# A four-layer graph network: ranking by source and the first node stage with their work in another order

## The reference

```python
h_in = relu(layernorm(x))                      # then the layer's own products
# layer 0
h_raw = h_in @ W.T + b
h_dir = h_raw / max(norm(h_raw), 1e-12)
h     = h_dir * sigmoid(h_in @ mag_w.T + mag_b) * 1.5
scores = h[src] @ a_s + h[tgt] @ a_t           # one number an edge
ex  = exp(scores - segment_max(scores, tgt)[tgt])
agg = segment_sum(h[src] * ex / (segment_sum(ex, tgt)[tgt] + 1e-10), tgt)
h   = ball_projection(h + agg)
```

## Time and profile before

| | |
|---|---|
| median of three runs | 9786.06 us |
| profiled execution, its span | 9778.72 us, 9777.0 us |
| busy share of the span | PE 62%, DVE 58%, POOL 50%, ACT 32% |
| granted TensorE clock, mean | 0.80 of full speed |
| first node stage | about 130 to 929 us of the span |
| ranking by source | about 933 to 2129 us |

### The profile page before, as it was taken

The page is one execution under the profiler, slowest core; times in us unless marked ns, Lnnn a source line. Parts: engine busy times, 40 slices in busy tenths (PEclk is TensorE's granted clock), DMA queues, the critical chain, the costliest instruction groups (busy, mean ns, idle before and its releaser), DMA issues. The chain is left out here.

```text
span 9777.0 us, 155051 instructions
## 1 busy us (share of the span) xinstructions
PE 6076.9 (62%) x21338; PEld 3661.3 (37%) x21339; DVE 5653.9 (58%) x19482; ACT 3099.9 (32%) x10799; POOL 4876.5 (50%) x5997
## 2 busy tenths in 40 slices
PE   4666877756768887677999945444003678500277
PEld 3554233324543433455666611111002557400165
DVE  4666988873558776354445455555001458755664
ACT  2665022211554443254444400000000466411046
POOL 1333177756632212664444467775666652455252
PEclk8998577777989998799999966666556999755599
DMA  2332000004876654596666632332002797411057
GB/s 84 134 132 96 0 1 1 1 1 151 284 256 215 214 206 173 181 302 233 236 234 234 222 98 90 91 90 66 1 0 76 234 302 217 144 42 42 23 178 229
DMA packets 779248, 1347.62 MB, mean 138 GB/s; under 512 B 139839, under 2 KB 546391, under 8 KB 779156
## 3 DMA queue, kind: packets, MB, share of 16 engines
q1 hardware_dynamic: 208564, 650.10, 19.0%
q10 hardware_dynamic: 413792, 410.91, 13.2%
q0 software_dynamic: 156800, 285.65, 10.5%
HBM read 751.95 MB, written 594.32 MB: 138 GB/s over the span
## 5 line engine op out<-in xcount | busy, mean ns | idle before, releaser
L1435 PE MATMUL node_p_out<-w,node_h_t 128*128 128x512 f32 (+3 forms) x7840 | 2614.7, 466 | 379.1 <-ACT node_h_t L1463 141.9
L990 PE MATMUL merge_banks<-merge_rows,merge_mask 128*128 x6264 | 1680.7, 425 | 744.0 <-SPq L959 464.5
L1435 PEld LDWEIGHTS node_p_out<-w,node_h_t 128*128 128x128 f32 x7840 | 1357.1, 197 | 1077.7 <-issue 734.9
L990 PEld LDWEIGHTS merge_banks<-merge_rows,merge_mask 128*128 128x128 f32 x6264 | 1278.1, 211 | 1146.6 <-issue 954.0
L972 DVE TENSOR_SCALAR merge_mask<-ramp,dst_at,soft_at_step 128x128 f32<-128x128 f32 x2349 | 847.2, 366 | 1069.8 <-PE merge_banks L990 950.3
L1078 POOL DMA_INDIRECT merge_rows<-h,merge_take_i x1176 | 1125.1, 957 | 655.6 <-issue 249.4
L1022 ACT COPY merge_total<-merge_banks 128x256 f32<-128x256 f32 x1568 | 577.6, 369 | 1251.5 <-PE merge_banks L990 1135.4
L1613 PE MATMUL score_table<-score_at_high,score_at_low 128*128 128x392 f32 x784 | 565.6, 827 | 588.8 <-DVE score_at_high L1574 584.0
L1009 ACT COPY merge_banks<-merge_held 128x256 f32<-128x256 f32 x1568 | 588.1, 376 | 897.5 <-DMA merge_held<-own 643.3
L1353 POOL TENSOR_TENSOR node_inv_std<-node_var,node_minus_half 128x4 f32<-128x4 f32 x392 | 437.0, 1115 | 751.0 <-DVE node_var L1311 750.0
L1463 ACT ACTIVATE node_h_t<-node_p_turn 128x256 f32<-128x256 f32 x1568 | 594.7, 385 | 349.6 <-PE node_p_turn L1413 344.9
(11 more groups left out here) (409 smaller groups left out, 9678.3 us busy)
## 6 DMA issues: line engine op xcount, KB each, us to landing
h<-node_out SPq DMA_DIRECT2D x196, 512.0 KB, 5.7
merge_held<-own ACTq DMA_DIRECT2D x196, 512.0 KB, 5.8
x<-merge_total ACTq DMA_DIRECT2D x196, 512.0 KB
node_x<-x SPq DMA_DIRECT2D x196, 512.0 KB, 5.9
node_x<-in_x SPq DMA_DIRECT2D x194, 512.0 KB
h<-node_rows_h SPq DMA_DIRECT2D x98, 512.0 KB, 2.7
merge_held<-h ACTq DMA_DIRECT2D x98, 512.0 KB
mix<-merge_total ACTq DMA_DIRECT2D x98, 512.0 KB
```

Of the source, the lines that this page charges most:

```text
L990: nc.tensor.matmul(banks[:, bass.ds(nc.s_assert_within(at[2 * j + 1], 0, (BANKS - 1) * 512, skip_runtime_bounds_check_because=small), D)], ...
L1435: ins = nc.tensor.matmul(p_out[w][g % banks][:, 0:n], h_t[g][:, c * P:(c + 1) * P], matrix[:, c, :], start=c == 0, stop=c == 1)
```

## The change

Node stage, layer 0: DVE's and ACT's stages are called tile by tile (`by_tile=True`): one tile of each stage, then the next tile of each. `normalize` comes first, then `add_bias`, then `average`. `resize` follows two steps after `measure` instead of one. The pair columns are scaled by one DVE instruction a group (`pair_tile`, L1509 after) in place of four of ACT's; SP waits for it before it stores.

Ranking: `rank_sources` takes the place of `rank_phase` with `EndSums`. The 392 low one-hots are kept from the histogram. The running starts live in one PSUM bank: PE adds into it, ACT copies it out (`snap`) before each addition. Engines work on different tiles in one step: DVE high one-hot of tile t, mask of t-2, pick of t-4; PE add of t-2, transpose of t, match of t-1, rank of t-3. POOL copies its own indices, eight tiles at once, gathers, and adds the pairs itself.

```diff
+def rank_sources(nc, k, pos_out, ends, score):
+    ph = Phase(nc, "rank_src")
...
+    p_run = ph.ps("run", [P, 512])
...
+            def hot_low(t, j):
+                nc.vector.tensor_scalar(at_low[:, bass.ds(t, 1), :].rearrange("p o f -> p (o f)"), k.ramp[:, 0:P],
+                                        columns(low, t), None, ALU.is_equal).then_inc(hist_low, 1)
+            def hot_high(t, j, done):
+                nc.vector.tensor_scalar(at_high[j][:], k.ramp[:, 0:NTH], columns(high, t), None, ALU.is_equal).then_inc(done, 1)
+            def histogram(t, j):
+                hot_low(t, j)
+                after(dve, hist_mm, t - U + 1)
+                hot_high(t, j, hist_high)
...
+            def head(t, j):
+                after(dve, ranked, t - U + 1)
+                after(dve, added, t - U + 1)
+                after(dve, picked_n, t - U + 1)
+                hot_high(t, j, high_hot)
+            def before_in_tile(t, j):
+                dve.wait_ge(same, t + 1)
+                after(dve, ranked, t - FOUR + 1)
+                nc.vector.tensor_tensor(earlier[j % FOUR][:], p_same[j % 2][:, 0:P], k.before[:],
+                                        ALU.mult).then_inc(masked, 1)
+            def pick(t, j):
+                dve.wait_ge(ranked, t + 1)
+                dve.wait_ge(high_hot, t + 1)
+                after(dve, picked_n, t - 1)
+                if j == 0 and not (isinstance(t, int) and t < U):
+                    dve.wait_ge(rank_kept, t // U if isinstance(t, int) else (t >> 3))
+                nc.vector.tensor_tensor_reduce(picked[j % 2][:], at_high[j][:], p_rank[j % 2][:, 0:NTH], 1.0, 0.0,
+                                               ALU.mult, ALU.add, rank_f[:, j:j + 1]).then_inc(picked_n, 1)
+                if j == U - 1:
+                    dve.wait_ge(picked_n, t + 1)
+                    nc.vector.tensor_copy(columns(pos_out, t - U + 1, U), rank_f[:]).then_inc(rank_kept, 1)
+            walk(dve, [(0, head), (2, before_in_tile), (4, pick)])
...
+            def add(t, j):
+                pe.wait_ge(high_hot, t + 1)
+                pe.wait_ge(snapped, t + 1)
+                nc.tensor.matmul(p_run[:, 0:NTH], at_low[:, bass.ds(t, 1), :].rearrange("p o f -> p (o f)"), at_high[j][:],
+                                 start=False, stop=False, skip_group_check=True).then_inc(added, 1)
...
+            def rank(t, j):
+                pe.wait_ge(copied, t + 1)
+                pe.wait_ge(snapped, t + 1)
+                after(pe, picked_n, t - 1)
+                nc.tensor.matmul(p_rank[j % 2][:, 0:NTH], low_t[j][:], starts[j % FOUR][:], start=True, stop=False)
+                pe.wait_ge(masked, t + 1)
+                pe.wait_ge(high_hot, t + 1)
+                nc.tensor.matmul(p_rank[j % 2][:, 0:NTH], earlier[j % FOUR][:], at_high[j][:], start=False,
+                                 stop=True).then_inc(ranked, 1)
+            walk(pe, [(2, add), (0, turn), (1, match), (3, rank)])
+        @block.scalar
+        def _(act):
+            act.wait_ge(prefix, 1)
+            def snap(t, j):
+                after(act, added, t)
+                after(act, ranked, t - FOUR + 1)
+                nc.scalar.copy(starts[j % FOUR][:], p_run[:, 0:NTH]).then_inc(snapped, 1)
+            def copies(t, j):
+                act.wait_ge(turned, t + 1)
+                after(act, same, t - FOUR + 1)
+                nc.scalar.copy(low_tb[j % FOUR][:], p_turn[j % 2][:, 0:P]).then_inc(copied_b, 1)
+                after(act, ranked, t - U + 1)
+                nc.scalar.copy(low_t[j][:], p_turn[j % 2][:, 0:P]).then_inc(copied, 1)
+            walk(act, [(2, snap), (0, copies)])
...
+            def block_of(i, half, uses):
+                at = half * U
+                nc.gpsimd.tensor_copy(take_src[:, at:at + U], columns(k.src_i, i * U, U)).then_inc(indexed, 1)
+                nc.gpsimd.tensor_copy(take_dst[:, at:at + U], columns(k.dst_i, i * U, U)).then_inc(indexed, 1)
+                pool.wait_ge(indexed, 2 * (i + 1))
+                pool.sem_inc(turn_pool, 1)
+                for j in range(at, at + U):
+                    nc.gpsimd.indirect_dma_start(of_src[:, j, :], None, ends,
+                                                 bass.IndirectOffsetOnAxis(take_src[:, j:j + 1], 0)).then_inc(got[half], 16)
+                    nc.gpsimd.indirect_dma_start(of_dst[:, j, :], None, ends,
+                                                 bass.IndirectOffsetOnAxis(take_dst[:, j:j + 1], 0)).then_inc(got[half], 16)
+            def join(i, half, uses):
+                at = half * U
+                pool.wait_ge(got[half], 16 * 2 * U * uses)
+                nc.gpsimd.tensor_tensor(columns(score, i * U, U), of_src[:, at:at + U, 0], of_dst[:, at:at + U, 1],
+                                        ALU.add).then_inc(scored, 1)
+                pool.wait_ge(scored, i + 1)
+                pool.sem_inc(turn_pool, 1)
...
+        live = []
         for lag, stage in stages:
             side = (c - lag) % S
             uses = i + (c - lag - side) // S
             H = uses * S + side
             if isinstance(H, int) and not 0 <= H < groups:
                 continue
-            stage(Group(H, side, uses, groups))
+            live.append((stage, Group(H, side, uses, groups)))
+        for g in range(G if by_tile else 1):
+            for stage, q in live:
+                stage(q, g) if by_tile else stage(q)
...
+                    sp.sem_inc(turn_sp, 1)
+                    sp.wait_ge(paired, q.H + 1)
...
+            def normalize_tile(q, g):
+                if g == 0:
+                    dve.wait_ge(std_made, q.H + 1)
+                    if not q.new:
+                        dve.wait_ge(turned, G * q.last)
+                ins = nc.vector.tensor_scalar(xn[q.h][:, g, :], x[q.h][:, g, :], moments[q.h][:, g, 0:1],
+                                              inv_std[q.h][:, g:g + 1], ALU.subtract, ALU.mult)
+                if g == G - 1:
+                    ins.then_inc(normed, 1)
+            def bias_tile(q, g):
+                if g == 0 and not q.new:
+                    dve.wait_ge(out_made, q.last)
+                    dve.wait_ge(paired, q.last)
+                dve.wait_ge(product, G * q.H + g + 1)
+                nc.vector.tensor_tensor(out[q.h][:, 0, g, :], p_out[0][g][:, 0:n_out], k.bias0[:], ALU.add).then_inc(raw_made, 1)
+            def pair_tile(q, g):
+                if g < G - 1:
+                    return
+                dve.wait_ge(scale_made, q.H + 1)
+                if not q.new:
+                    dve.wait_ge(t_put[q.h], 16 * n_put * q.i)
+                nc.vector.tensor_tensor(pair_h[q.h][:], out[q.h][:, 0, :, D + 1:D + 3],
+                                        scale[q.h][:].rearrange("p (g o) -> p g o", o=1).to_broadcast([P, G, 2]),
+                                        ALU.mult).then_inc(paired, 1)
...
-                pipeline(dve, groups, [(norm_lag, normalize), (0, average), (after_lag, add_bias)])
+                pipeline(dve, groups, [(norm_lag, normalize_tile), (after_lag, bias_tile), (0, average_tile),
+                                       (after_lag + 2, pair_tile)], by_tile=True)
...
+            def measure_tile(q, g):
+                act.wait_ge(raw_made, G * q.H + g + 1)
+                if not (q.first and g < 2):
+                    act.wait_ge(squared, G * q.H + g - 1)
+                if g == 0 and not q.new:
+                    act.wait_ge(scale_made, q.last)
+                nc.scalar.activation(junk[g % 2][:], out[q.h][:, 0, g, 0:D], ACT.Square,
+                                     accum_out=size2[q.h][:, g:g + 1]).then_inc(squared, 1)
+                if g == G - 1:
+                    act.wait_ge(squared, G * (q.H + 1))
+                    nc.scalar.activation(gate[q.h][:], out[q.h][:, 0, :, D], ACT.Sigmoid).then_inc(gated, 1)
+            def resize_tile(q, g):
+                if g == 0:
+                    act.wait_ge(scale_made, q.H + 1)
+                    if not q.new:
+                        act.wait_ge(t_put[q.h], 16 * n_put * q.i)
+                ins = nc.scalar.activation(rows_h[q.h][:, g, :], out[q.h][:, 0, g, 0:D], ACT.Copy, scale=scale[q.h][:, g:g + 1])
+                if g == G - 1:
+                    ins.then_inc(out_made, 1)
...
+                pipeline(act, groups, [(work_lag, rectify_tile), (after_lag, measure_tile), (after_lag + 2, resize_tile)],
+                         apart=2, by_tile=True)
```

More of the change, by code:

```diff
@@ L1510, in _, with rectify_tile @@
-            pipeline(act, groups, {
-                0: [(work_lag, work), (after_lag, measure), (after_lag + 1, resize)],
-                1: [(0, squares), (1, bound), (work_lag, work)],
-            }.get(layer, [(work_lag, work)]), apart=2)
+            def rectify_tile(q, g):
+                if q.first and g == 0:
+                    rectify(q, 0)
+                if g + 1 < G:
+                    rectify(q, g + 1)
+                elif not q.final:
```

(1 more changed line is left out.)

256 lines of the change are left out of this document (137 added, 119 removed).

## The result

The changed kernel takes 9562.4 us (median of 4 runs, 9552.17 to 9566.03), the kernel before 9784.88 us in the same job (9775.1 to 9792.57): ratio 0.977, 95% interval 0.9755 to 0.9788, a gain of 222 us. The forecast was 9532 us, with a range of 9465 to 9625. The profiled execution has a span of 9564.3 us, 212.7 less than before.

A forecast was written before the change was run, and what follows sets the result against it. POOL's gathers were taken to bound the ranking, and waits between engines the node stage. From 9778.7 us profiled, 144 us off the ranking and 105 off the node stage gave 9530, stated as 9532; range 9465 to 9625.

The forecast's parts named there:

- POOL's chain: Ranking: POOL's gathers start with the phase instead of after the histogram and end it near 1983 us; 144 us less.
- a seam: Ranking, between POOL's gather blocks: addition, index copies and their waits cost 1.31 us more than the usual 0.30, 48 times.
- Cover by the other engines: Ranking: PE, DVE and ACT finish the second loop near 1780 us, about 1.5 us a tile, leaving POOL last by 200 us.
- Rival B: Ranking's second loop: PE stays at 1.2 GHz, 2.35 us a tile, so the ranking gains 19 us: 9655 us; chance 0.06.
- Who pays beside a gather: Ranking's histogram: DVE's one-hot beside a gather goes from 0.41 to 0.61 us, while the gather stays at 0.94 us.
- rival C: Ranking: POOL waits for DVE, 0.2 us a gather, 157 us in all, taking the ranking's gain: 9686 us; chance 0.05.
- Node stage: Layer 0's node stage: DVE's ring sets a pitch of 6.75 us a group instead of 7.85; 105 us less.
- The passage: Node stage, once a group: fourth normalization, transpose, last product and its bias addition cannot overlap; 1.53 us.
- lower bound: Node stage: no gain but ACT's pairs off its queue, about 0.3 us for each of 97 groups, about 30 us.
- clock dips: Node stage: 0.30 us a group kept for PE's slower clock, since PE's pause shrinks only from 2.88 to about 2 us.
- rival A: Node stage without gain: waits for PE hold up DVE and ACT, groups stay near 7.5 us: 9605 us; chance 0.14.
- D: Ranking's second loop: the single bank serializes, 4.6 us a tile, deciding from 2.67, so slower: 10537 us; chance 0.04.

The follow-up runs named there:

- e3: The changed kernel with POOL held until the histogram's prefix sums before its first gather: 9775.88 us, ratio 0.9988 to the kernel before.
- e4: The kernel before with its old ranking walk, but POOL making its own index copies, gathers and additions, eight tiles a block: 9730.75 us, ratio 0.9943.
- f1: The changed kernel itself, run again on chip 15: 10269.88 us against 10340.73 for the kernel before there, ratio 0.9929.
- e7: The changed kernel with each node-stage normalization signalled, so PE transposes a tile once that one is normalized: 10105.38 us on chip 12, ratio 0.9771 to the kernel before.
- e5: The kernel before, order by group kept, with only the pair columns moved to one DVE instruction a group: 10231.88 us on chip 12, ratio 0.9894.
- f2: The kernel before with only the pair columns moved to one DVE instruction a group, repeated on chip 15: 10228.53 us, ratio 0.9892.
- e2: The changed ranking with the node stage of the kernel before, on chip 0: 9655.48 us, ratio 0.9868 to the kernel before.

## Why the prediction was right, and where not

**POOL's chain: right, and shown.** The head start is the gain (e3), within a block gathers follow at 0.30 us, and a seam costs 1.49 us more than that on average, put at 1.31. The size was 144 us and is 119 in the profile after. The chain was put at 1983 - 933.5 = 1049.5 us and took 1898.3 - 820.6 = 1077.7. Adding up POOL's rows, those 28 us are: the first gather, 1.9 us late; the gathers' own length, 5 us; the 48 seams, 8 us; and the other gaps, 13 us. The gathers, before and after (count, busy us and mean ns, idle time before):

```profile
L455 POOL DMA_INDIRECT rank_src_of_src<-ends,rank_src_take_src x392 | 371.2, 947 | 340.9 <-ACT rank_src_take_dst L435 228.7 <-issue 93.9 <-DVE soft_score L463 17.7
L457 POOL DMA_INDIRECT rank_src_of_dst<-ends,rank_src_take_dst x392 | 370.4, 945 | 119.5 <-issue 98.8 <-DVE soft_score L463 10.4 <-ACT rank_src_take_dst L435 9.5
```

```profile
L573 POOL DMA_INDIRECT rank_src_of_src<-ends,rank_src_take_src x392 | 378.4, 965 | 145.8 <-issue 107.1 <-POOL rank_src_take_dst L569 38.7
L575 POOL DMA_INDIRECT rank_src_of_dst<-ends,rank_src_take_dst x392 | 373.6, 953 | 130.4 <-issue 130.4
```

752.0 against 741.6 us is 10 us, of which the forecast had put 5 in the first gather and the first of each block. The gaps within blocks have 13 us more than 0.30 each, 11 of it in six pauses such as the one at 980.10, 112 gathers or about 154 us apart, which the kernel before did not have. They come with POOL's own program (e4); what in it makes them I don't know. The gathers' price came from a stretch in which few stood beside histogram one-hots: in the changed kernel a gather takes 0.967 us on average beside the histogram, 0.962 beside the second loop and 0.947 alone. The bounds (104 to 165 us) covered all this.

**Cover by the other engines: right on this chip.** Picks were to end near 1780 in the old offset, 1189 + 590, or about 847 us after the phase began; they end 817 after. The tile takes 1.44 us, forecast 1.5. e4 shows that the cover was needed: with the old walk the gain is 56 us. Rival B's condition (1.2 GHz in that loop) didn't come about: the granted clock is 1.00.

**Who pays beside a gather: true where it was read, not elsewhere.** DVE paid and POOL hardly did (0.02 us a gather, not the 0.2 of rival C), as I took from the earlier trace rows, so rival C fell. The 0.61 in place of 0.41 us that I carried over the whole histogram held there: 331 tiles in 200 us (835 to 1035) is 0.60 us a tile, as forecast. On chips 12 and 15 DVE loses four fifths of its time in the same loop, and the ranking's part turns into a cost. Nothing in the trace of before hinted at that, and a forecast of "9532 us" was one for the kind of chip that the trace came from. The rule of the Trainium skill (SBUF — State Buffer, Who interferes with whom), that the one instruction that issued first holds the other off for its whole length, would give at most one gather, 0.94 us, for an instruction of DVE, if the ports are free when the gather ends. The first chip's 0.2 us is well under that. f1's idle times, 489.0 / 239 = 2.05 us before a high one-hot and 278.5 / 246 = 1.13 before a low one, are over it, and they begin only after 15 us of work beside gathers at full speed. What holds DVE there stays open: I have not told ports, the supply of instructions and other causes apart.

**Node stage: the time right, the mechanism half right.** Forecast 105 us, measured 112 in the trace and 116 by the medians; pitch 6.75 against 6.66. The passage is real and e7 removes it. What was wrong is the account of the kernel before: "PE sat 2.88 us until the first addition freed a bank", with ACT's queue priced only as a lower bound, "about 0.3 x 97 = 30 us". e5 gains 105 us by the pairs alone. The step failed in the reading of the earlier trace rows: the bank had been free for 5.9 us, the wait bears the name of the semaphore that moved last, and PE waited for ACT's relu, behind the pairs. Read so, the pairs are worth their 0.75 us a group, 73 us from the 7.52 us groups; the rest of e5's 105 goes with the higher clock, 1.00 in f2's stretch of 500 to 600 against 0.91. That the forecast came out even so is in the main not luck: it went from the measured 7.85 to a pitch built from DVE's load and the passage, and neither term used the wrong reading. The 0.30 us for clock dips was a guess, of which 0.21 was needed. The lower bound and rival A did rest on the wrong reading. The passage was put at 1.53 us, and taking it away gave 1.78. What the forecast did not weigh is that one of its two edits, the pairs on DVE, costs 18 us in tile order.

**Rivals A and D** did not occur: groups were not near 7.5 us, and a tile of the second loop takes 1.44 us, not the 2.67 at which D would decide.

## What to carry to other kernels

When an engine checks two counts before an instruction, the name in the wait is that of the one that moved last and need not be the one that was missing: read in the code which count it asks for, and see whose name the same wait bears in other groups. Here four short instructions, 0.75 us together, on the engine that was not named were worth 105 us. Look for the one hand-over that is made per group where it could be made per tile; here three signals more took 180 us off. And an overlap of DVE with POOL's gathers is to be timed on more than one chip before it is counted on.

## What the runs showed of the hardware

- The same code takes 9785 us on chips 0 and 2 and 10342 us on chips 12 and 15. The node stage lasts the same on all. For the changed kernel 605 of the 727 us between the two profiled spans (9564.3 and 10291.2) lie in the ranking (1680 against 1075 us), where DVE and gathers run side by side.
- POOL can pause for 2.2 us in a row of gathers, every 112 gathers or about 154 us, with nothing waited for: six times each in the changed kernel, e2, e3 and e4; the 776 gathers of the kernel before that followed its histogram had no such pause.
- The granted clock did not follow PE's busy share: over 500 to 600 us of the node stage it was 0.91 with PE busy 66 in the kernel before, 0.93 with 74 in the changed one, 1.00 with 68 in f2, where PE's longest pause in a group is 2.13 us in place of 2.88.
